# GpSimd takes part in the end of a feed-forward: state sums and a steady term ahead of the last product, and two output blocks shared by ScalarE and VectorE

## What is computed

```python
global_context = x.mean(axis=1, keepdims=True)
gf = _global_net(global_context, ...)            # one number per sequence
out = x
for _ in range(NUM_CYCLES):                      # 3
    tf = _coupling_net(out, ...)                 # one number per token
    combined = 0.7 * gf + 0.3 * tf
    coupling = BASE_COUPLING + adaptive_range * (combined - 0.5) * 2.0
    out = out + coupling * _twist(out)           # _twist: feature halves swapped, with signs
# and outside:  result = _layernorm(x + out)
```

## Time and profile before

| | |
|---|---|
| median of 3 runs | 283.04 us (281.01 to 283.7) |
| span of the profiled execution, first to last instruction | 280.2 us |
| mean granted TensorE clock | 0.970 |
| PE busy | 251.0 us, 90% of the span |
| PEld busy | 110.9 us, 40% |
| DVE busy | 200.2 us, 71% |
| ACT busy | 234.9 us, 84% |
| POOL busy | 81.4 us, 29% |

### The profile page before, as it was taken

How to read it: one execution, slowest core, us unless ns; L and a number is a source line. 1 busy time by engine, 2 the same in 40 slices (tenths; PEclk the granted TensorE clock), 3 DMA queues, 4 the chain that set the end, 5 groups by cost and what they waited for, 6 DMA issues and landing times.

```text
span 280.2 us, 8439 instructions
## 1 busy us (share of the span) xinstructions
PE 251.0 (90%) x2959; PEld 110.9 (40%) x2960; DVE 200.2 (71%) x760; ACT 234.9 (84%) x339; POOL 81.4 (29%) x241
## 2 busy tenths in 40 slices
PE   8249899999999999999999999989898999999990
PEld 3033334434344343443434444434343332223890
DVE  1687588696886967869678696773254477999993
ACT  3147899999999999999999999999975777788685
POOL 8540422415234152241522415320111000000473
PEclk9757999999999999999999999999999999999997
DMA  5201751753516526155351650615300175653045
GB/s 130 56 1 20 95 113 36 102 100 92 112 29 140 102 48 150 32 99 106 81 112 37 132 109 23 131 41 91 67 13 0 37 153 121 135 121 74 1 137 165
DMA packets 58072, 23.43 MB, mean 84 GB/s; under 512 B 42785, under 2 KB 56001, under 8 KB 58049
## 3 DMA queue, kind: packets, MB, share of 16 engines
q1 hardware_dynamic: 57760, 23.11, 39.1%
q10 hardware_dynamic: 288, 0.02, 0.1%
HBM read 4.90 MB, written 2.10 MB: 25 GB/s over the span
## 4 chain that ended last, share of the span: by engine, by line
PE 69%; issue 12%; ACT 9%; DVE 4%; DMA 2%; POOL 1%; ACTq 0%; DVEq 0%; POOLq 0%
PE O L589 11%; PE O L595 10%; PE S L713 8%; PE S L502 5%; PE S L512 4%; ACT o_sb L888 3%; PE M L628 3%; PE M L614 3%; PE S L531 3%; PE S L754 2%; DMA qk<-parts 2%; PE S L492 2%; PE S L522 2%; PE M L639 2%; PE S L723 2%
## 5 line engine op out<-in xcount | busy, mean ns | idle before, releaser
L882 ACT ACTIVATE probs_past<-S 128x1024 f32<-128x1024 f32 x64 | 64.5, 1038 | 7.1 <-PE S L492 7.1
L882 ACT ACTIVATE probs_late<-S 128x1024 f32<-128x1024 f32 x64 | 66.4, 1050 | 1.3 <-PE S L502 1.3
L589 PE MATMUL O<-probs_past,values 128*32 128x512 f32 x256 | 34.8, 612 | 7.0 <-ACT o_sb L888 5.8
L882 ACT ACTIVATE probs_early<-S 128x1024 f32<-128x1024 f32 x32 | 32.8, 1027 | 3.7 <-PE S L531 3.7
L595 PE MATMUL O<-probs_late,values 128*32 128x256 f32 x512 | 34.3, 385 | 0.2
L1130 DVE TENSOR_TENSOR roped<-rotated,rstd 128x128 f32<-128x128 f32 (+1 forms) x64 | 12.2, 247 | 26.7 <-POOL rstd L1506 26.5
L1491 POOL TENSOR_TENSOR minus_half_sum<-sum_eps,minus_half 128x40 f32<-128x40 f32 x16 | 4.5, 283 | 80.5 <-DVE estimate L1118 74.8
L1367 DVE SCALAR_TENSOR_TENSOR cY<-coup,ratio,Y 128x256 f32<-128x256 f32 x48 | 21.1, 481 | 5.8 <-ACT coup L966 5.0
L713 PE MATMUL S<-X,cn_w 128*128 128x512 f32 x48 | 25.0, 627 | 0.0
L502 PEld LDWEIGHTS S<-qk 32*64 32x64 bf16 x512 | 8.0, 101 | 34.0 <-issue 34.0
L502 PE MATMUL S<-qk 32*64 32x256 bf16 x512 | 20.2, 292 | 0.2 <-ACT probs_late L882 0.2
(11 more groups left out here) (185 smaller groups left out, 528.1 us busy)
## 6 DMA issues: line engine op xcount, KB each, us to landing
Y<-X SPq DMA_DIRECT2D x48, 128.0 KB, 2.4
xT_in<-in_xT SPq DMA_DIRECT2D x16, 128.0 KB, 2.6
x_res<-in_x SPq DMA_DIRECT2D x16, 128.0 KB, 2.1
out<-result SPq DMA_DIRECT2D x16, 128.0 KB, 1.9
qk<-parts SPq DMA_TRANSPOSE x15, 4.9
future_in<-in_future SPq DMA_DIRECT2D x1, 128.0 KB, 2.7
w_o<-in_w_o SPq DMA_DIRECT2D x2, 64.0 KB, 2.6
cn_w<-in_cn_w SPq DMA_DIRECT2D x2, 64.0 KB, 2.8
```

What stands on the lines that cost most here:

```text
L589: mm = pe.matmul(O[32 * g:32 * g + 32, :], values[p][:, 0, g, s, at:at + 32], probs_past[:, s, g, :], start=m == 0, stop=False)
L882: act.activation(dst, S[TILE_BUFFER[n]][:, :, :], ACT.Exp).then_inc(exp_done[n], 1)
```

## The change

POOL adds the state after u=3 to `X0` for half 1 (`add_far_states`), then computes `ratio * Y * local_gain` into a new tile `steady_part` and adds it to `X0` too (`add_steady_part`). TensorE's `turn_states` turns only `X0`, after a wait for POOL's sums, and VectorE's cY of u=5 is the plain product `coup * Y`, one operation of 512 columns. Block 6, too, is shared: chunks 0 and 1 are written by VectorE (`store_low`), chunks 2 and 3 by ScalarE, from the PSUM bank of block 0 for block 6 and of block 1 for block 7. In the branch of the attention for unbounded gains two pairs of semaphores are merged. Both roots and new work share POOL's queue in the order written at the end.

```diff
             bank = BACK_BANKS[f - 6 if f in SHARED_OUTPUTS and t >= 2 else f]      # before: 0 if f == 7 and t >= 2 else f
...
             for f in range(8):
                 sp.wait_ge(n_["result_ready"], f + 1)
-                if f == 7:
-                    sp.wait_ge(n_["last_ready"], 1)
+                if f in SHARED_OUTPUTS:
+                    sp.wait_ge(n_["low_result_ready"], f - 5)
...
                     if general:
-                        pe.wait_ge(n_["q0_ready_max"], b + 1)
-                        pe.wait_ge(n_["q1_ready_max"], b + 1)
+                        pe.wait_ge(n_["q_ready_max"], (b + 1) * T)
...
             def turn_states(f):
                 pe.wait_ge(tanh_done[f - 4], 2 * CYCLES)
-                if f == 7:
-                    pe.wait_ge(n_["result_ready"], 1)
+                pe.wait_ge(n_["far_steady_done"], f // 2 * 4 - 4)
+                if f in SHARED_OUTPUTS:
+                    pe.wait_ge(n_["result_ready"], f - 5)
                 for t in range(4):
-                    fresh = t == 0 or f == 7 and t == 2
+                    fresh = t == 0 or f in SHARED_OUTPUTS and t == 2
                     pe.matmul(back_chunk(f, t), chunk(X0, f, t), ident[:, :], start=fresh, stop=False)
-                    pe.matmul(back_chunk(f, t), chunk(X, f, t), ident[:, :], start=False, stop=False)
...
-            for f in range(7):
-                store_normalized(f)
-            store_normalized(7, range(2, 4))
+            for f in range(8):
+                store_normalized(f, range(2, 4) if f in SHARED_OUTPUTS else range(4))
...
+                if u == 2 * CYCLES - 1:
+                    dve.tensor_tensor(cY[:, j, :].rearrange("p (a n) -> p a n", a=2), coup[:, j, :].rearrange("p (a n) -> p a n", a=2),
+                                      block(Y), ALU.mult).then_inc(cY_done[j], 1)
+                    return
...
-            def store_last():
-
+            def store_low(f):
+
+                dve.wait_ge(n_["f_rstd_done"], f + 1)
+                dve.wait_ge(stored[f % 4], 32)
                 for t in range(2):
-                    last = dve.tensor_scalar(result[:, 3, t, :], back_chunk(7, t), f_mom[:, 7, t, 0:1],
-                                             f_rstd[:, 7, t:t + 1], ALU.subtract, ALU.mult)
-                last.then_inc(n_["last_ready"], 1)
+                    last = dve.tensor_scalar(result[:, f % 4, t, :], back_chunk(f, t), f_mom[:, f, t, 0:1],
+                                             f_rstd[:, f, t:t + 1], ALU.subtract, ALU.mult)
+                last.then_inc(n_["low_result_ready"], 1)
...
+            for f in range(1, 8):
+                if f <= 4:
+                    add_turned(5, 1, f - 1)
                 stats_of(f)
                 shift_of(f - 1)
-            dve.wait_ge(stored[3], 32)
+                if f == 7:
+                    store_low(6)
             shift_of(7)
-            store_last()
+            store_low(7)
...
+            def add_far_states(j):
+
+                u = 2 * CYCLES - 3
+                block = lambda tile: block_of(tile, 1, j, leaves_spread(u))
+                pool.wait_ge(X_done[j], u + 1)
+                pool.tensor_tensor(block(X0), block(X0), block(X), ALU.add).then_inc(n_["far_sums_ready"], 1)
+
+            def add_steady_part(j):
+
+                u = 2 * CYCLES - 1
+                pool.wait_ge(n_["ratio_ready"], 2)
+                for i in range(2):
+                    pool.wait_ge(Y_loaded[1][j // 2 * 2 + i], 32 * (u // 2))
+                if j > 0:
+                    pool.wait_ge(n_["far_steady_done"], 2 * j)
+                for n, b in enumerate(block_batches(j, leaves_spread(u))):
+                    last = pool.tensor_scalar(steady_part[:, n, :], block_of(Y, 1, j, leaves_spread(u))[:, n, :],
+                                              ratio[:, 8 + b:9 + b], local_gain[:, :], ALU.mult, ALU.mult)
+                last.then_inc(n_["far_steady_done"], 1)
+                pool.wait_ge(n_["far_steady_done"], 2 * j + 1)
+                pool.wait_ge(n_["far_sums_ready"], j // 2 * 2 + 2)
+                block = block_of(X0, 1, j, leaves_spread(u))
+                pool.tensor_tensor(block, block, steady_part[:, :, :], ALU.add).then_inc(n_["far_steady_done"], 1)
...
+            for j in range(4):
+                add_far_states(j)
+            for j in range(4):
+                add_steady_part(j)
+            for f in range(8):
+                root_of(f)          # the two operations of lines 1545 and 1547, as before
```

More of the change, by code:

```diff
@@ L240, in block_kernel @@
         cY = sb("cY", [128, 4, 512])
+        steady_part = sb("steady_part", [128, 2, SEQ])
         f_stats = sb("f_stats", [128, 8, 4, 6])
@@ L256, in back_chunk @@
         def back_chunk(f, t):
-            bank = BACK_BANKS[0 if f == 7 and t >= 2 else f]
+            bank = BACK_BANKS[f - 6 if f in SHARED_OUTPUTS and t >= 2 else f]
             return bank[:, t * 128:(t + 1) * 128]
@@ L270, in block_kernel @@
                  "block_part_done block_scored block_max_done max_step_done max_parts_ready "
-                 "q0_turned_max q1_turned_max q0_ready_max q1_ready_max "
+                 "q_turned_max q_ready_max "
                  "q0_turned q1_turned k_turned q0_ready q1_ready k_ready qk_turned "
@@ L276, in block_kernel @@
                  "h3_done gelu3_done "
-                 "gain_diag_ready sums_ready turned_back f_stats_done f_moments_done f_var_done f_rstd_done f_shift_done result_ready last_ready").split()
+                 "gain_diag_ready sums_ready far_sums_ready far_steady_done turned_back f_stats_done f_moments_done f_var_done f_rstd_done f_shift_done result_ready low_result_ready").split()
         n_ = {n: sem(n) for n in names}
@@ L420, in turn_queries @@
                                       parts[:, u:u + G, :, :].rearrange("p u s d -> p (u s d)"), ident16[:, :])
-                mm.then_inc(n_[f"q{t}_{turned}"], 1)
+                mm.then_inc(n_[f"q{t}_turned"] if turned == "turned" else n_["q_turned_max"], 1)
             def turn_first_keys():
@@ L808, in turn_product @@
                 for t in range(4):
-                    whole = t == 3 or f == 7 and t == 1
+                    whole = t == 3 or f in SHARED_OUTPUTS and t == 1
                     mm = pe.matmul(back_chunk(f, t), cY[:, f - 4, t * 128:(t + 1) * 128], gain_diag[:, :], start=False, stop=whole)
@@ L1185, in copy_queries @@
             def copy_queries(b, p, t):
-                dve.wait_ge(n_[f"q{t}_turned_max"], b + 1)
+                dve.wait_ge(n_["q_turned_max"], b * T + t + 1)
                 dve.tensor_copy(qT[p][:, t, :, :, :].rearrange("p r s n -> p (r s n)"), MAX_TURN_BANKS[t][:, :])\
-                   .then_inc(n_[f"q{t}_ready_max"], 1)
+                   .then_inc(n_["q_ready_max"], 1)
             def subtract_maximum(b, p):
@@ L1369, in add_turned @@
                 last.then_inc(cY_done[j], 1)
-                if u == 2 * CYCLES - 1:
-                    return
                 dve.wait_ge(cY_done[j], u + 1)
@@ L1539, in _, with root_of @@
                  ln_rstd[:, :], n_["ln_rstd_ready"])
-            for f in range(8):
+            def add_far_states(j):
[18 more added lines that the diff above has]
+                pool.tensor_tensor(block, block, steady_part[:, :, :], ALU.add).then_inc(n_["far_steady_done"], 1)
+            def root_of(f):
                 pool.wait_ge(n_["f_moments_done"], f + 1)
@@ L1547, in _ @@
                 pool.tensor_tensor(f_rstd[:, f, :], f_var[:, f, :], minus_half[:, 0:4], ALU.pow).then_inc(n_["f_rstd_done"], 1)
+            for j in range(4):
[4 more added lines that the diff above has]
+                root_of(f)
 FFN_LOADS = 17
+SHARED_OUTPUTS = (6, 7)
 ORDER = list(range(128)) + list(range(192, 256)) + list(range(128, 192))
```

## The result

| | before | changed |
|---|---|---|
| median of six runs | 282.74 us (281.01 to 283.7) | 290.4 us (289.21 to 291.63) |
| ratio, 95% interval | | 1.0266 (1.023 to 1.0301) |
| span of the profiled execution | 280.2 us | 289.7 us |
| mean granted TensorE clock | 0.970 | 0.955 |

What follows compares the result with a forecast made beforehand. VectorE was taken to bound the end, nearly without air from 254.07 us on. Collision +9.2 and lighter tail -1.2 gave +8.0 on the median 283.04: 291.0 us, range 282 to 294.5.

Steps and rivals of the forecast that it cites:

- A: POOL's operations at these sizes do not collide with VectorE's, leaving only the gain of 1.2 us: 281.8 us; chance 0.15.
- B: POOL and VectorE share the port in small bits, 3 us of POOL's work at no cost: +5.5, 288.5 us; chance 0.12.
- The collision: From 247.8 to 260.40 us, POOL's reads and VectorE's SBUF operations take turns; VectorE's first statistics start 9.2 us later.
- the 16 fit between these 23: POOL's 16 new operations all run between VectorE's 23 before its first statistics, each pushing VectorE by its read; sum 10.1 us.
- POOL is done by then, its roots are not late: When VectorE's delayed first statistics start, POOL has finished its new work, so its roots add no delay.
- rival C: No collision, but slow POOL makes the first root late, 2.9 us beyond its room: +1.7, 284.7 us; chance 0.06.
- Rival D: The collision, plus a lower TensorE clock in the tail as TensorE waits between pieces: +1 more, 292 us; chance 0.1.
- The lighter tail: After the first statistics: TensorE's wait 0.26, plain multiplications 0.75, ScalarE's lighter end 0.2; together 1.2 us less.
- (a): VectorE's X and cY operations from 248 to 270 us last up to 1 us longer, in turns with POOL's.
- (b): VectorE's first statistics, `stats_of(0)`, start near 269.6 us.
- (c): From VectorE's first statistics to the last result takes 15.3 us, where it took 16.5.
- (d): POOL's additions last about 1.1 us, more where they wait.

Runs made afterwards that it cites:

- e4: The kernel before plus eight idle POOL additions of 128x512 on tiles nobody else uses; 291.61 us, ratio 1.0302.
- e5: The kernel before plus eight idle POOL memsets of 1536 columns, which write and read nothing; 283.2 us, ratio 1.0028.
- e9: The changed kernel plus 16 matmuls on zeros between product 4 and state block 6, where TensorE had waited; 289.62 us, ratio to before 1.0245.
- e2: The changed kernel without POOL's 16 operations and the wait for them, its result incomplete; 281.65 us, ratio to before 0.994.
- e1: The changed kernel with POOL's last steady part cut in three and roots 0 to 2 between the pieces; 291.95 us, ratio to before 1.0323.
- e11: The changed kernel with roots between last steady part's pieces, products 5 and 6 before state blocks 6 and 7, 16 matmuls on zeros before state block 6; 289.59 us.

## Why the prediction was right, and where its steps were not

**The total.** 291.0 us forecast, 290.4 measured; by the stretches +8.0 forecast, +8.7 measured. That the total came so near is in part luck, as the sum at the end of this section shows. The mechanism that decided it, a port taken in turns whole operation by whole operation, was right: rivals A (no collision) and B (shared in small bits) are out, by e4, and by pairs that lose 1.01 us and not less. The Trainium skill says it of GpSimd's reads and not of its writes ("SBUF — State Buffer", Who interferes with whom), and e5 bears that out at 1536 columns. It has the lock held for the whole instruction, as the prediction says; here the measured loss is less, 1.01 us beside an addition that takes 1.26 alone, and 0.35 beside a scaling that takes 0.70.

**The collision was mis-sized, 9.2 forecast, 6.5 measured.** The large read was right: 0.97 forecast, 1.01 measured. The small one, 256 columns from one input, I took at 0.30 us; it costs 0.10 to 0.18, 0.14 on average, so eight would cost 1.1 and not 2.4. And "the 16 fit between these 23" was wrong. Each of POOL's first four additions waits for its block of X, for 1.15 us three times, so the twelve operations of the steady part can begin only at 258.55, when twelve of VectorE's are left. For 0.25 us of an addition (1.26 alone, 1.01 lost) and for 0.2 of hand-over to the next scaling POOL does not hold VectorE up, VectorE gets on in between, and the blocks of the steady part start 3.6 to 3.7 us apart. It reached its statistics with the third part's addition under way and the whole fourth part still to do. By VectorE's rows the loss is 4.1 us in u=3 and its additions and 2.75 in u=4, less 0.36: 6.5. That is six additions in place of eight, 6.0 us, and six scalings, 0.86. The 0.5 us that I had allowed for VectorE's own waits for cY do not show.

**"POOL is done by then, its roots are not late" failed.** POOL ended 4.2 us after the first statistics began. I had priced a late root as rival C, without a collision; in fact collision and late root came together. It shows as 2.39 us before the first shift, `f_shift` waiting for POOL, which was the prediction's own sign of rival C. By e9 and e2 this late work costs 2.24 us. But e1 shows that the root's place in the queue alone is not the cause: state block 6 needs POOL's last addition, and taking roots forward makes that later.

**"TensorE and ScalarE wait for VectorE, so nothing else is" failed in part.** Rival D was there, 1 us by its sum, 0.84 by e9. It came with TensorE's wait of 3.85 us in the tail (filling that wait removed it) and not with the small waits between its pieces that I had named.

**The lighter tail was nearly right**: 1.2 forecast, 0.90 in e2. ScalarE's relief was 0.14 and not 0.2. The saving of 0.19 us for each plain product came in two blocks of four: in e2 VectorE's first five statistics follow each other after 1.96, 2.05, 1.86 and 2.05 us, and before after 2.17, 2.04, 2.06 and 2.05. In the others POOL's `f_var` lasts longer behind the plain product, 0.63 to 0.72 us in place of 0.20 to 0.42, and the shift waits for that root.

So three errors nearly cancelled, and that was luck: 2.7 us too much for the collision, against 3.1 for the tail (18.73 against 15.65 of e2) and 0.3 for the gain. A forecast of the approach and the tail, each by itself, would have been off by 2.7 and 3.4 us. Of the four signs that the prediction named for itself, (a) came true, (b) and (c) did not (the first statistics at 268.06 and not 269.6, and 1.2 of that from before the change; the tail at 18.73 and not 15.3), and (d) is near: 1.26 us where nothing disturbed an addition, not 1.1.

## What to carry to other kernels

Before moving element work from a full VectorE to an idle GpSimd, count the columns that GpSimd would read while VectorE runs operations with two SBUF inputs: here each addition of 512 columns, 1024 read, cost VectorE 1.01 us, more than the 0.60 in which VectorE would have done it itself. Of what ran beside POOL here, statistics read from PSUM lost nothing, and POOL's pure writes cost nothing: such pairs are the ones to look for. And when moved work comes late, look at all that is queued behind it and who needs it: here taking the first waiter forward gave nothing until TensorE's order and clock were mended too.

## What the runs showed of the hardware

- VectorE lost 1.01 us to a POOL addition of 512 columns, 0.35 to a scaling of 512, and 0.10 to 0.18 to one of 256, but nothing to a memset of 1536 columns. The scaling of 512 lasted 0.70 us on POOL, so it held VectorE up for half of its time; the addition lasted 1.26 us alone and held it up for 1.01.
- A VectorE operation on four columns with both inputs in SBUF waited 1.06 us behind a POOL addition (e11).
- Statistics read from PSUM kept their 0.88 us beside POOL scalings, and so did the four small `bn_aggr` behind them, with one input in SBUF, their 0.38 us (270.76 in the changed kernel). No larger VectorE operation with a single SBUF input ran beside POOL, so for such a one nothing is shown.
- In the stretches around and after TensorE's wait of 3.85 us its granted clock was 0.67 and 0.65; with 16 idle matmuls in that wait (e9) it was 1.00. In e4, after a stretch in which it was busy for 2.76 us of 6, it was 0.53.
